# Attention in 64x32 TensorE tiles: scores and projections in four column strips, value sums in two key halves

## The reference

```python
x = x + attention(layernorm(x))          # 32 heads of 16, w_q, w_k, w_v, w_o
x = x + ffn(layernorm(x))
# attention
q, k, v = (proj(w) for w in (w_q, w_k, w_v))       # (b, heads, s, 16)
attn = softmax(q @ k.T / sqrt(16))                  # 64 score matrices of 1024 x 1024
out = (attn @ v).reshape(b, s, 512) @ w_o.T
# ffn: ternary weights (512 -> 1376 -> 512), int4 activations in, int8 inside
inter = int8_quant(up(xq) * relu(gate(xq)) ** 2)
y = down(inter)
```

## Time and profile before

| | |
|---|---|
| median of 3 runs | 962.65 us (962.37 to 963.83) |
| the profiled execution | 963.78 us, of which the traced span is 962.0 us |
| TensorE matmuls (PE) | busy 894.6 us, 93% of the span |
| VectorE (DVE) | busy 847.1 us, 88% |
| ScalarE (ACT) | busy 750.3 us, 78% |
| GpSimd (POOL) | busy 233.8 us, 24% |
| granted TensorE clock, mean over the span | 0.987 |

### The profile page before, as it was taken

One profiled execution on the slowest core, in us unless ns is written; L12 is line 12 of the kernel. 1 busy time (PEld: TensorE's weight loads), 2 busy tenths in 40 slices (PEclk: granted clock), 3 DMA queues, 4 the chain that ended last, 5 costly groups with the idle time before them and its releaser, 6 DMA issues.

```text
span 962.0 us, 17694 instructions
## 1 busy us (share of the span) xinstructions
PE 894.6 (93%) x6232; PEld 294.7 (31%) x6232; DVE 847.1 (88%) x1576; ACT 750.3 (78%) x1468; POOL 233.8 (24%) x367
## 2 busy tenths in 40 slices
PE   4799999999999999999999999999999998999986
PEld 3333222222222222222222222222222224454442
DVE  6877799999999999999999999999999667788975
ACT  4422499888888898899888888888888976777784
POOL 3600011162111111821363431421043222000000
PEclk9989899999999999999999999999999998999999
DMA  8340021121114122331413223141231202111000
GB/s 308 88 161 2 1 54 42 40 56 41 40 34 125 51 88 56 97 100 34 107 45 87 60 81 85 27 113 48 78 122 35 57 20 73 65 46 45 22 34 33
DMA packets 40573, 64.96 MB, mean 68 GB/s; under 512 B 5926, under 2 KB 20774, under 8 KB 40486
## 3 DMA queue, kind: packets, MB, share of 16 engines
q1 hardware_dynamic: 40486, 63.85, 23.2%
HBM read 42.27 MB, written 21.23 MB: 66 GB/s over the span
## 4 chain that ended last, share of the span: by engine, by line
PE 46%; DVE 31%; ACT 10%; issue 6%; DMA 3%; SPq 2%; POOL 1%; ACTq 0%; DVEq 0%; POOLq 0%
DVE mx L1008 22%; PE ps L490 16%; PE ps L410 12%; PE ps L469 8%; ACT PB L775 5%; PE ps L326 5%; DVE XV L1105 2%; PE ps L606 2%; PE ps L635 1%; PE ps L570 1%; ACT XV L845 1%; DMA tu<-wkT 1%; DVE hm L1114 1%; ACT XV L840 1%; ACT PB L856 1%
## 5 line engine op out<-in xcount | busy, mean ns | idle before, releaser
L1008 DVE TENSOR_REDUCE mx<-ps 128x1 f32<-128x512 f32 x1024 | 636.6, 683 | 44.4 <-PE ps L410 42.3
L775 ACT ACTIVATE PB<-ps 128x512 f32<-128x512 f32 x1024 | 537.4, 606 | 77.5 <-PE ps L469 76.3
L410 PE MATMUL ps<-QK 48*128 48x512 f16 x1024 | 334.9, 384 | 27.9 <-DVE mx L1008 23.5
L469 PE MATMUL ps<-QK 50*128 50x512 f16 x1024 | 314.1, 385 | 4.0 <-ACT PB L775 1.4
L490 PE MATMUL ps<-PB,Vg 128*32 128x512 f32 x2048 | 273.3, 606 | 0.0
L410 PEld LDWEIGHTS ps<-QK 48*128 48x128 f16 x1024 | 89.2, 94 | 309.2 <-DVE mx L1008 232.0
L388 PE MATMUL ps<-XV,wqk 64*128 64x512 f16 x624 | 160.6, 377 | 0.0
L469 PEld LDWEIGHTS ps<-QK 50*128 50x128 f16 x1024 | 76.4, 94 | 109.0 <-ACT PB L775 84.8
L1272 POOL TENSOR_SCALAR nmb<-nm 128x16 f16<-128x16 f32 x32 | 6.5, 203 | 366.8 <-DVE nm L1013 366.5
L845 ACT ACTIVATE XV<-XV,magic,hm 128x512 f32<-128x512 f32 (+1 forms) x48 | 33.5, 760 | 40.0 <-DVE hm L1130 40.0
L490 PEld LDWEIGHTS ps<-PB,Vg 128*32 128x32 f32 x2048 | 40.7, 108 | 66.2 <-issue 44.8
(11 more groups left out here) (164 smaller groups left out, 787.2 us busy)
## 6 DMA issues: line engine op xcount, KB each, us to landing
parts_d<-spl SPq DMA_DIRECT2D x64, 128.0 KB
att_d<-OS SPq DMA_DIRECT2D x32, 256.0 KB
XV<-x SPq DMA_DIRECT2D x28, 256.0 KB, 5.3
QK<-parts_d SPq DMA_DIRECT2D x48, 128.0 KB, 2.6
QK<-parts_d SPq DMA_DIRECT2D x16, 256.0 KB, 4.2
XV<-att_d SPq DMA_DIRECT2D x8, 512.0 KB, 3.4
XV<-rden_d SPq DMA_DIRECT2D x8, 512.0 KB, 4.7
out<-PB SPq DMA_DIRECT2D x16, 256.0 KB, 2.0
```

What stands on the lines that cost most here:

```text
L410: nc.tensor.matmul(ps[:, at % S_BANKS, :], QK[rows, sup % 2, 2 * set_ + p, 0, half * HALF + qt * P:half * HALF + (qt + 1) * P], QK[rows, s ...
L469: nc.tensor.matmul(ps[:, T_BANK + t_slot(n) % T_BANKS, :], QK[rows, sup % 2, 2 * set_ + p, 1, kt * P:(kt + 1) * P], QK[rows, sup % 2, 2 * ...
L775: nc.scalar.activation(PB[:, at % 3, 2 * (i // 2) + t_side(step, i), :], ps[:, T_BANK + t_slot(n) % T_BANKS, :], ACT.Exp, scale=exp_reg).t ...
L1008: nc.vector.tensor_reduce(mx[:, v % 2, idx, kh:kh + 1], ps[:, at % S_BANKS, :], AX.X, ALU.max).then_inc(s_used, 1)
```

## The change

Three things change, and nearly only in the units of attention up to 29:

- **Strips.** Every item and T of these units and every piece is issued as four matmuls of 32 columns (`STRIP`, `STRIPS` = 4), each with its own weight load and into its own 32 partitions of the same bank, with the same 512 moving columns. Only the last of the four signals. The items before the first super-unit and the T of units 30 and 31 stay in one piece.
- **Value sums in halves.** `pe_av` is called twice a step, for 64 keys each: first on side `first_side(step)`, right behind the first T, then on the other side late in the step. The second half adds into the same bank and waits for the first (`av_half`). In units 30 and 31 it stays whole.
- **Order and sides.** The items' sides in steps 1 and 2, the T's sides in steps with r = 2 and the order within a step change, so that items and T on one side stand behind each half of the value sums on the other. The third T (index 3) stands behind two pieces.

```diff
-SCORE_SIDES = ((0, 0, 0, 0), (1, 0, 0, 1), (1, 0, 0, 1), (1, 1, 1, 1), (0, 0, 0, 0), (1, 1, 1, 1), (0, 0, 0, 0), (1, 1, 1, 1))
+SCORE_SIDES = ((0, 0, 0, 0), (1, 1, 1, 0), (0, 0, 0, 1), (1, 1, 1, 1), (0, 0, 0, 0), (1, 1, 1, 1), (0, 0, 0, 0), (1, 1, 1, 1))
...
-            last = nc.tensor.matmul(ps[:, job_bank(n), :], stationary, moving, start=first_piece, stop=last_piece)
+            for c in range(STRIPS):
+                strip = slice(c * STRIP, c * STRIP + STRIP)
+                last = nc.tensor.matmul(ps[strip, job_bank(n), :], stationary[:, strip], moving, start=first_piece, stop=last_piece)
...
-            nc.tensor.matmul(ps[:, at % S_BANKS, :],
-                             QK[rows, sup % 2, 2 * set_ + p, 0, half * HALF + qt * P:half * HALF + (qt + 1) * P],
-                             QK[rows, sup % 2, 2 * set_ + p, 1, kh * HALF:(kh + 1) * HALF],
-                             start=True, stop=True).then_inc(s_psum, 1)
+            width = P // strips
+            for c in range(0, P, width):
+                last = nc.tensor.matmul(ps[c:c + width, at % S_BANKS, :],
+                                        QK[rows, sup % 2, 2 * set_ + p, 0, half * HALF + qt * P + c:half * HALF + qt * P + c + width],
+                                        QK[rows, sup % 2, 2 * set_ + p, 1, kh * HALF:(kh + 1) * HALF],
+                                        start=True, stop=True)
+            last.then_inc(s_psum, 1)
...
-            return SIDES[i] if step % KEYT in (1, 2, 3, 5, 7) else 1 - SIDES[i]
+            return SIDES[i] if step % 2 else 1 - SIDES[i]
...
-            nc.tensor.matmul(ps[:, T_BANK + t_slot(n) % T_BANKS, :],
-                             QK[rows, sup % 2, 2 * set_ + p, 1, kt * P:(kt + 1) * P],
-                             QK[rows, sup % 2, 2 * set_ + p, 0, half * HALF:(half + 1) * HALF],
-                             start=True, stop=True).then_inc(st_psum, 1)
-
-        def pe_av(pe, sup, step):
+            width = P // strips
+            for c in range(0, P, width):
+                last = nc.tensor.matmul(ps[c:c + width, T_BANK + t_slot(n) % T_BANKS, :],
+                                        QK[rows, sup % 2, 2 * set_ + p, 1, kt * P + c:kt * P + c + width],
...
+        def first_side(step):
+            return 1 - step % 2
...
-            if kt == 0:
+            if kt == 0 and side in (None, first_side(step)):
...
+            if side is None:
+                for h in range(GH):
+                    last = nc.tensor.matmul(ps[32 * h:32 * h + 32, av_bank(at), :], Vg[:, set_, kt, h, :],
+                                            PB[:, (sup * STEPS + step) % 3, h, :], start=(kt == 0), stop=(kt == KEYT - 1))
+                last.then_inc(av_done, 1)
...
+            second = side != first_side(step)
+            if second:
+                pe.wait_ge(av_half, sup * STEPS + step + 1)
+            rows = slice(side * SIDE, side * SIDE + SIDE)
             for h in range(GH):
-                last = nc.tensor.matmul(ps[32 * h:32 * h + 32, av_bank(at), :], Vg[:, set_, kt, h, :],
-                                        PB[:, (sup * STEPS + step) % 3, h, :], start=(kt == 0), stop=(kt == KEYT - 1))
-            last.then_inc(av_done, 1)
+                last = nc.tensor.matmul(ps[32 * h:32 * h + 32, av_bank(at), :], Vg[rows, set_, kt, h, :],
+                                        PB[rows, (sup * STEPS + step) % 3, h, :], start=(kt == 0 and not second),
+                                        stop=(kt == KEYT - 1 and second))
+            last.then_inc(av_done if second else av_half, 1)
 
...
+            def lagging(step, side):
+                if step > 1:
+                    pe_av(pe, sup, step - 2, side)
+                elif sup > 0:
+                    pe_av(pe, sup - 1, STEPS - 2 + step, side)
...
-                elif r in (1, 2):
-                    item(step, 0)
-                    pe_scoresT(pe, sup, step, 0)
-                    item(step, 1)
-                    item(step, 2)
-                    pe_scoresT(pe, sup, step, 1)
-                    item(step, 3)
-                    pe_scoresT(pe, sup, step, 2)
-                    pe_scoresT(pe, sup, step, 3)
+                    pe_scoresT(pe, sup, step, 2, 1)
+                    pe_scoresT(pe, sup, step, 3, 1)
+                    lagging(step, None)
                 else:
-                    item(step, 0)
-                    pe_scoresT(pe, sup, step, 0)
-                    pe_scoresT(pe, sup, step, 1)
-                    piece(0)
-                    item(step, 1)
-                    piece(1)
-                    item(step, 2)
-                    piece(2)
-                    pe_scoresT(pe, sup, step, 2)
-                    piece(3)
-                    pe_scoresT(pe, sup, step, 3)
-                    item(step, 3)
-                if step > 1:
-                    pe_av(pe, sup, step - 2)
-                elif sup > 0:
-                    pe_av(pe, sup - 1, STEPS - 2 + step)
+                    first = first_side(step)
+                    if r in (1, 2):
+                        item(step, 0)
+                        pe_scoresT(pe, sup, step, 0, STRIPS)
+                        lagging(step, first)
+                        item(step, 1)
+                        pe_scoresT(pe, sup, step, 1, STRIPS)
+                        item(step, 2)
+                        pe_scoresT(pe, sup, step, 2, STRIPS)
+                        pe_scoresT(pe, sup, step, 3, STRIPS)
+                        item(step, 3)
+                        lagging(step, 1 - first)
+                    else:
+                        item(step, 0)
+                        pe_scoresT(pe, sup, step, 0, STRIPS)
+                        lagging(step, first)
+                        item(step, 1)
+                        pe_scoresT(pe, sup, step, 1, STRIPS)
+                        item(step, 2)
+                        pe_scoresT(pe, sup, step, 2, STRIPS)
+                        item(step, 3)
+                        piece(0)
+                        lagging(step, 1 - first)
+                        piece(1)
+                        pe_scoresT(pe, sup, step, 3, STRIPS)
+                        piece(2)
+                        piece(3)
```

More of the change, by code:

```diff
@@ L44 @@
 HALF_RANGE = 32768.0
+STRIP = 32
+STRIPS = P // STRIP
 EXPONENT = 0x7F800000
@@ L230, in build @@
         st_psum, probs, av_done = sem("st_psum"), sem("probs"), sem("av_done")
+        av_half = sem("av_half")
         os_copy, os_out = sem("os_copy"), [sem(f"os_out{r}") for r in range(2)]
@@ L392, in pe_job_half, with pe_scores @@
                 last.then_inc(job_turn, 1)
-        def pe_scores(pe, sup, unit, k):
+        def pe_scores(pe, sup, unit, k, strips):
             qt, p, side, kh = item_of(sup * 4 + unit, k)
@@ L454, in pe_max_rows, with pe_scoresT @@
             last.then_inc(rows_psum, 1)
-        def pe_scoresT(pe, sup, step, i):
+        def pe_scoresT(pe, sup, step, i, strips):
             unit, kt = step // KEYT, step % KEYT
@@ L468, in pe_scoresT, with pe_av @@
             rows = slice(side * SIDE, side * SIDE + AUG)
-            nc.tensor.matmul(ps[:, T_BANK + t_slot(n) % T_BANKS, :],
-                             QK[rows, sup % 2, 2 * set_ + p, 1, kt * P:(kt + 1) * P],
-                             QK[rows, sup % 2, 2 * set_ + p, 0, half * HALF:(half + 1) * HALF],
-                             start=True, stop=True).then_inc(st_psum, 1)
-        def pe_av(pe, sup, step):
+            width = P // strips
+            for c in range(0, P, width):
+                last = nc.tensor.matmul(ps[c:c + width, T_BANK + t_slot(n) % T_BANKS, :],
+                                        QK[rows, sup % 2, 2 * set_ + p, 1, kt * P + c:kt * P + c + width],
+                                        QK[rows, sup % 2, 2 * set_ + p, 0, half * HALF:(half + 1) * HALF],
+                                        start=True, stop=True)
+            last.then_inc(st_psum, 1)
+        def first_side(step):
+            return 1 - step % 2
+        def pe_av(pe, sup, step, side):
             unit, kt = step // KEYT, step % KEYT
@@ L488, in pe_av @@
                     pe.wait_ge(rows_used, 1)
+            if side is None:
[3 more added lines that the diff above has]
+                last.then_inc(av_done, 1)
+                return
+            second = side != first_side(step)
+            if second:
+                pe.wait_ge(av_half, sup * STEPS + step + 1)
+            rows = slice(side * SIDE, side * SIDE + SIDE)
             for h in range(GH):
-                last = nc.tensor.matmul(ps[32 * h:32 * h + 32, av_bank(at), :], Vg[:, set_, kt, h, :],
-                                        PB[:, (sup * STEPS + step) % 3, h, :], start=(kt == 0), stop=(kt == KEYT - 1))
-            last.then_inc(av_done, 1)
+                last = nc.tensor.matmul(ps[32 * h:32 * h + 32, av_bank(at), :], Vg[rows, set_, kt, h, :],
```

(17 more changed lines are left out.)

4 lines of the change are left out of this document (removed).

## The result

The changed kernel took 982.7 us (median of 4 runs, 980.32 to 983.09); the kernel before took 962.93 us beside it (962.37 to 963.83). The ratio is 1.0199, with a 95% interval of 1.0181 to 1.0217: **2.0% slower**. 945 us and a faster kernel were forecast, from 935 to 990. The profiled execution has a span of 981.0 us against 962.0, 19.0 longer.

A forecast was written before the change was run, and what follows sets the result against it. VectorE, 94 to 96% full, bounds attention, with TensorE neck and neck. Of 27.3 us of waits, less 4.9, 3.0 and 1.8, the change wins 17.6: 963.8 - 17.6 - 1.1 = 945 us, range 935 to 990.

The forecast's parts named there:

- Does VectorE see the slack?: Between steps, the next item may start 1.42 us after the last and would need 1.13; 0.17 us waiting left per unit.
- queue rival: Second passes of each half block matmuls behind them, so the other row half idles: about 1009 us, chance 0.15.
- supply rival: TensorE instructions come too slowly, deciding from 19 ns each: 986 us at 22 ns, 1106 at 27; chance 0.10.
- The waits of the maxima, 25.0 to 5 to 9: Sign of being right: VectorE's maxima in units 1 to 29 wait 5 to 9 us for scores instead of 25.0.
- The bound of 27.3 us: Most the change can give: maxima's waits for scores, 25.0 us in units 1 to 29 plus 2.3 in unit 0.
- the sum: Gain in attention: 27.3 us of waits less 4.9 left in units, 3.0 for `act_abs` units, 1.8 in unit 0: 17.6.
- ScalarE as slack, not loss: Outside the `act_abs` units ScalarE works 17.93 of 20.70 us; its 65.3 us of waits for T cost nothing.
- The floor after, 2.24 us: TensorE's shortest step with pieces after the change: T 0.22, two halves of 0.91, 0.20 between them; VectorE needs 2.48.
- The hand-over: Between the two halves of the value sums, completion seen and second half started: 0.20 us.
- second passes: In the value sums, the second float32 passes start 0.45 us after the first.
- Strips at nothing: Four times the instructions for items, T and pieces cost nothing; strips run beside each other, three banks hide 18 ns.
- That the slack would not reach VectorE: Rival: completion between the halves costs 0.45 us, not 0.20, so VectorE's waits stay; about 958 us, chance 0.13.

The follow-up runs named there:

- run 3: Changed kernel with item 1 issued ahead of the first half of the value sums in every step: 961.91 us, ratio 1.0004 to the kernel before.
- run 10: run 8's kernel with item 0 behind the first half of the value sums as well: 1113.52 us, ratio 1.1549 to the kernel before.
- run 1: Kernel before with items, T and pieces in four strips, its order and whole value sums kept: 968.44 us, ratio 1.0068.
- run 8: Changed kernel with VectorE's reciprocal of the softmax sums one step later (r = 7 instead of r = 6): 974.43 us, ratio 1.0136.
- run 5: run 3's kernel with VectorE's reciprocal of the softmax sums one step later: 955.04 us, ratio 0.9925 to the kernel before.
- Run 11: run 5's kernel with item 3 ahead of T 3 in the steps r = 1 and 2: 953.02 us, ratio 0.9889 to the kernel before.
- run 6: Kernel before with VectorE's reciprocal of the softmax sums one step later and nothing else: 959.97 us, ratio 0.9971.
- run 2: Changed kernel with items, T and pieces in one piece of 128 columns, order and halves kept: 2183.41 us, a single run.

## Why the prediction was wrong

**The step that failed** is "Does VectorE see the slack?". It let the next item be seen 0.39 + 0.05 us after its own start, and looked at the last item of a step and the first of the next alone. That holds for an item with nothing longer ahead of it in the program. Behind a first half, item 1 is seen when the half's last pass has ended. In the step r = 3 it was seen 1.72 us after its start (224.06 to 225.78). Three banks allow the next item to start 1.42 us after the last; the delay that counts is that of the signal, and the change put five of a step's tiles behind a 1.1 us matmul group. Moving one item ahead of the half took some 20 us off (run 3), moving another behind it added 139 (run 10).

The measured 982.7 us lies inside the stated 935 to 990. That is luck: the part above 966 was left for the queue and supply rivals, and neither is what happened.

**The rule was on the page that I cited.** I weighed the Trainium skill's rule (TensorE: Matmul & The Clock Gate, Part 3, "The mechanism") that matmuls start in order, and gave it 0.15 as the queue rival. The same rule says that they also end in order, and I passed over that half. The trace disagrees with the first half: item 1 started 0.54 us ahead of the passes before it. For the second half the signals agree: all nine above come in program order, though by the modelled ends item 1 had streamed 1.22 us before the first half.

**The waits of the maxima, 25.0 to 5 to 9.** They rose to 33.0, and they were the wrong gauge: in run 3, some 20 us faster, they are still 28.8. In the typical unit 0.25 us more shows as pauses and the rest as maxima that lie less close: thirteen take 8.36 us, which is (8.36 - 0.68) / 12 = 0.640 from one to the next, when run 3 has (7.27 - 0.68) / 11 = 0.599. The starts of all maxima of units 1 to 29 give the better gauge. Their median distance is 0.598 us in each trace named here. Where a maximum starts within 0.06 us of its score's signal, what the distance has above 0.598 is lateness of that score. It adds up to 43.3 us before, 48.5 with strips alone (run 1), 58.9 in the changed kernel, 37.2 in run 3, 59.1 in run 8 and 37.8 in run 5. From before to the changed kernel that is 15.6 more, and from run 8 to run 5 21.3 less, beside 19.4 us of the kernel's time.

**The bound of 27.3 us** was mis-sized for the same reason. I took 0.62 for VectorE's pace; with every score there in time it is 0.60. A score late by less than a tenth of a microsecond shows in no wait, only in this pitch: before it was (7.51 - 0.68) / 11 = 0.621. A unit of 20.71 us less 32 x 0.599, less the pauses of 0.65 and 0.11 for the negated maximum leaves 0.78: over 29 units some 23 us of lateness that the sum did not see; the count above gives 43.3 - 25.0 = 18. The best version still won only 10 us. (VectorE's share in attention was also read a little high: 20.35 of 21.90 us in unit 21 is 93%, not 94; nothing hangs on it.)

**ScalarE as slack, not loss.** With the change T 3 at r = 2 waits 0.58 us for ScalarE in every unit, 16.7 us in all, and TensorE stands idle meanwhile. The sum priced ScalarE only in the units with `act_abs`. Run 3's pause of 0.35 us stands right behind this wait. Run 11 moved the pause and did not remove it, and what the wait itself costs was not tried.

**The floor after, 2.24 us**, was right in its mechanism and small in size: from first half to first half it was 226.91 - 224.60 = 2.31 in unit 5. The hand-over was well priced: last pass ended 225.67, second half started 225.84, 0.17 against 0.20. The second passes follow 0.43 after the first, against 0.45.

**Strips at nothing** was wrong by about 6 us (run 1). The reasons given, that strips run beside each other and that banks hide 18 ns, fit the starts (for items 2 to 9 ns apart, the median 3) but not the signals.

**Left out altogether** was the DMA ahead of the reciprocal. The change touches none of its instructions. In unit 21, counted from the unit's start, ScalarE's copy of the value sums ended at 5.66 us before and 6.33 after, the DMA was issued at 16.76 and 17.62, and it landed 2.2 and 3.7 us later; what delays the issue and stretches the transfer stays open. It isn't item 1's place, nor the strips alone, with which the reciprocal waits 1.35, 0.96 and 0.76 us (run 1): in run 3 units 17, 21 and 25 are as long, 24.74, 24.89 and 23.86 us. The reading of the waits of before, where units 17, 21 and 25 already stood out at 22 us, would have asked for a price; it cost some 6 us, the half clock behind two of the waits included.

**The rivals.** The supply rival is refuted: 128 instructions a step came through in 2.31 us, 18 ns each, below the 19 from which it was to decide. One pause of 1.1 us before a value sum, in unit 9 (to 304.21 us), is of the kind "issue", and that unit is 1.2 us longer than unit 8. A late fetch fits it: the fetch packet nearest ahead started at 301.2, 8.0 us after the one before where the median is 5.6, and took 1.7 us, and from 303.10 to 304.15 the DMA engines show full (share 1.03). No run tests that. The queue rival has the right sign and place, and the wrong mechanism: scores do start beside a blocked half, and its 1009 us did not come. That the slack would not reach VectorE was right in words, but for the hand-over, which was not the cause, and its 958 was too good.

**Where the 20 us are**, then: strips some 6 (run 1); the reciprocal some 6 (runs 6 and 8); the held item 1 some 19 (run 8 against run 5). These make 31. The remainder of 11 the other way is what the halves and the new order gain once item 1 is not held; it is 960.0 + 6 - 955.0 (runs 6, 1 and 5), the number that closes the sum, and no run measures it by itself. The parts are differences of medians from different series of runs, good to 1 or 2 us each, and that they add is assumed.

## What to carry to other kernels

Tiles that ran beside each other on the array were still signalled in program order here. So a long matmul group belongs behind whatever a starving engine waits for, and what stands behind it should be what nobody needs soon: count the time to the signal, not to the end of the stream. When two engines run neck and neck, compute the pace of the second from its densest stretch, and look for units already longer than their neighbours: their hidden waits are the next to grow. And price a stall of TensorE with its clock: 3.4 us at half speed followed two of the three here.

## What the runs showed of the hardware

- A matmul group's signal waited for every group before it in the program (2396 of 2396 signals in order). Held signals come 0.059 us apart when each is for a tile of four strips, and no two were closer; with whole tiles the closest were 0.034 apart.
- Matmuls of 64x32 tiles can start ahead of one earlier in the program where their row halves differ (224.06 against 224.60 us). In the stretch of run 2 shown above, 64x128 tiles and 64x32 tiles did not.
- In run 2 the granted clock was 0.50 in attention, with TensorE shown busy for 100.00 of 100.00 us. A busy share near 100% did not mean full speed.
- Starts of an item's four strips lie 2 to 9 ns apart, and 128 TensorE instructions came through in 2.31 us.
- The granted clock was 0.50 for 3.4 us right behind TensorE gaps of 2.22 and 1.73 us, and stayed 1.00 behind one of 2.81 us.
- Maxima of 128x512 float32 from PSUM start 0.598 us apart back to back, though each lasts 0.68: lateness under a tenth of a microsecond shows in no wait.
